# The first two fifths of W_qkv split inside the last tile of the cross stage, in a shared buffer; W_o loads moved to later steps

## The chip, the cores and the metric

The kernel runs on one core of a Trainium2 chip. A time is the device time of one execution in microseconds; several executions are compared by their median. The engines are TensorE (PE), VectorE (DVE), ScalarE (ACT), GpSimd (POOL) and SyncE (SP, which here only issues DMAs and waits). The 16 DMA engines are shared by the queues that SP, ACT and POOL issue on.

## The reference

A decoder block on x (16 x 64 tokens, width 512), in float32: cross attention to a context, causal self attention, and a mixture of experts, each behind a layernorm and with a residual. Cut to the parts that matter here:

```python
def xattn(hq, kv_c):                      # 16 heads, context 1024 x 128
    q_r = einsum(einsum((hq @ Wq.T), w_kc_q), W_qr)
    kv_rope = kv_c * cos + rotate_half(kv_c) * sin
    attn = softmax(q_r @ (kv_rope @ W_kr).T)
    return ((attn @ kv_rope) @ w_kc_kv) @ Wo.T
def attn(h):                              # 32 query heads, 4 key/value heads of 64
    q, k, v = split(h @ w_qkv.T)          # w_qkv: (32 + 2 * 4) * 64 rows x 512
    q, k = rope(q), rope(k)
    return softmax(causal(q @ k.T * 64 ** -0.5)) @ v @ w_o.T
x = x + xattn(layernorm(x), ctx)
x = x + attn(layernorm(x))
x = x + moe(layernorm(x))                 # 16 experts, top 4 in 2 of 4 groups, and a shared one
```

## The kernel before, in words

The 1024 tokens are 8 tiles of 128 (two batches each). Four stages follow each other, each in a block of its own: every engine has a program of its own there, and all engines meet at the end of a block. `build_queries` folds the weights of the cross attention, `build_cross` does the cross attention and the layernorm behind it, `build_self` the self attention, `build_moe` the output projection and the experts. Products are made in three matmuls (`mm3`) of an upper and a lower float32r part. A `Pair` is such a split: ACT casts the raw data to the upper part, DVE or POOL subtracts it from the raw data for the lower one.

**The cross stage.** A tile is worked in four quarters c = 0 to 3 (two batches, two halves of the heads). In a quarter TensorE goes through k = 0 to 7: it turns the probabilities of key tile k into the PSUM banks psTr, two in turn; ACT casts them to the upper part (L653), DVE makes the lower part and so frees the bank (L700); two steps later TensorE multiplies them with the values (psV). Between these stand scores of the next quarter, where there is one, and heads of the output projection (psX). In the last quarter of the last tile there are no more scores, and behind its steps come heads 4 to 15, the residual, the layernorm of the last tile, its turn (L818), the cast and the store of h2 (L631). ACT issues the stores of x1 and h2. SP loads contexts and queries and fills the scatter area `xs` with zeros, 18 fills of 8 blocks. The last four fills are issued after the last tile's x load, and behind them, on the same queue, the loads of chunks 0 and 1 of W_qkv into the buffer `early`. At the end of its program ACT waits until all stores of x1 and h2 have landed.

**The self stage.** W_qkv has five chunks of 512 columns: chunk 0 for keys and values, 1 to 4 for the queries of four groups of heads. `high(c)` on ACT and `low(c)` on DVE split them. Chunk c + 1 is wanted by the c-th of the first steps. A step works one group of heads of one tile: products for three steps ahead, rope (three terms on DVE, a sum on POOL), the turn of the queries, scores, exponentials, the turn of the probabilities and the values. 32 steps are worked, the first 8 and the last 8 written out. SP loads h2 transposed (HT), the tables, chunks 2 to 4, and then chunks of W_o into the same raw buffers `ahead`, each behind the splitting of the chunk that lies there.

Of the kernel before, what the change touches and what calls it, by code (L numbers as in the profile page):

```python
# [29 lines left out]
P = 128  # L30
# [23 lines left out]


# [13 lines left out]
class Pair:  # L69
# [48 lines left out]
def build_queries(nc, ctx, sem, t, keep):  # L118
# [9 lines left out]
    WB = [Pair(ctx, nc, f"wb{j}", [P, W_B]) for j in range(2)]  # L128
    TW = sb("tw", [P, 2, R])
    C = Pair(ctx, nc, "cfold", [P, KC, P])  # L130
    Q = Pair(ctx, nc, "qr", [P, T])
# [73 lines left out]
    def _(pool):  # L205
# [25 lines left out]
    def _(act):  # L231
        def split_high(j, n):
            act.wait_ge(w_in[j], 16 * n)
            act.copy(WB[j].hi[:], raw[j][:, W_A:]).then_inc(wB_hi, 1)

# [183 lines left out]
TURN_H2_AT = (3, 2)  # L419

# [28 lines left out]
def build_cross(nc, ctx, sem, t, keep):  # L449
# [8 lines left out]
    KV = [Pair(ctx, nc, f"kv{j}", [P, LT, DC]) for j in range(2)]  # L458
    KT = [Pair(ctx, nc, f"kT{j}", [P, L]) for j in range(2)]
    QE = [ctx.enter_context(nc.sbuf_tensor(f"qe{j}", [P, 2, H * S], F32R)) for j in range(2)]  # L460
    PR = [sb(f"probs{j}", [P, RT, L]) for j in range(2)]
    PT = [Pair(ctx, nc, f"probsT{j}", [P, BANK]) for j in range(PTN)]
    CT = Pair(ctx, nc, "ctxT", [P, H, P])
# [25 lines left out]
    x1_out, h2_out = sem("x1_out"), sem("h2_out")  # L489
# [18 lines left out]

    block = ctx.enter_context(nc.Block())

    @block.sync
    def _(sp):
# [7 lines left out]
        def load_qe(b, j):  # L520
            sp.dma_start(QE[j][:].bitcast(F32), qe_d[b]).then_inc(qe_in[j], 16)
# [77 lines left out]
    def _(act):  # L599
# [4 lines left out]
        def kv_high(b, j):  # L604
            act.wait_ge(rope_done, b + 2)
            act.copy(KV[j].hi[:].rearrange("p l d -> p (l d)"), kr[j]).then_inc(kv_hi, 1)
# [76 lines left out]
        act.wait_ge(x1_out, 16 * NT + 16)  # L683
        act.wait_ge(h2_out, 16 * NT + 16)

    @block.vector
    def _(dve):
# [42 lines left out]

        def lo_k(j, q, count, slot):
# [146 lines left out]
WCH = 5  # L878
GI = 2 * HKV


def build_self(nc, ctx, sem, t, keep):
# [5 lines left out]
    W = Pair(ctx, nc, "wqkv", [P, WCH, KC, BANK])  # L888
    raw = keep["early"] + keep["ahead"][:WCH - 2]
    tab = sb("rope_s_tab", [P, 2, 3, DH // 2])  # L890
    mask_f, mask = sb("mask_f", [P, BANK]), sb("mask_r", [P, BANK], F32R)
    ident_r = sb("ident_r", [P, P], F32R)
    HT = [sb(f"h2T{j}", [P, 2, KC, P], F32R) for j in range(2)]
# [8 lines left out]
    VB = [Pair(ctx, nc, f"v_pairs{j}", [P, 2, HKV, 2, DH]) for j in range(2)]  # L902
    PR = [sb(f"sprobs{j}", [P, REP, S]) for j in range(2)]
    PT = [Pair(ctx, nc, f"sprobsT{j}", [P, REP // 2, P]) for j in range(2)]
# [14 lines left out]
    ht_in = [sem(f"ht_in{j}") for j in range(2)]  # L919
    w_hi, w_ready = sem("wqkv_hi"), sem("wqkv_ready")  # L920
# [39 lines left out]
    def _(sp):  # L960
        sp.dma_start(HT[0][:].bitcast(F32).rearrange("p a k x -> p a (k x)"), t["h2T"][0]).then_inc(ht_in[0], 16)
        sp.dma_start(tab[:], t["rope_s"]).then_inc(tab_in, 16)
        sp.dma_start(mask_f[:], t["mask"]).then_inc(tab_in, 16)
        for c in range(2, WCH):
            sp.dma_start(raw[c], t["w_qkv"][c]).then_inc(w_in[c], 16)
        sp.dma_start(HT[1][:].bitcast(F32).rearrange("p a k x -> p a (k x)"), t["h2T"][1]).then_inc(ht_in[1], 16)
        for c in range(W_AHEAD):
            if c < WCH - 2:
                sp.wait_ge(w_ready, c + 3)
            sp.dma_start(keep["ahead"][c], t["w_o"][:, c * KC:(c + 1) * KC, :]).then_inc(wo_in[c], 16)  # L970

# [66 lines left out]
    def _(act):  # L1038
        def high(c):
            act.wait_ge(w_in[c], 16)  # L1040
            act.copy(W.hi[:, c], raw[c]).then_inc(w_hi, 1)
# [38 lines left out]
        high(3)  # L1080
# [5 lines left out]
        def step(i, v, last):  # L1086
# [19 lines left out]
    def _(dve):  # L1106
# [21 lines left out]
        def low(c):  # L1128
            dve.wait_ge(w_hi, c + 1)
            dve.tensor_tensor(W.lo[:, c], raw[c], f32(W.hi[:, c]), ALU.subtract).then_inc(w_ready, 1)  # L1130
# [18 lines left out]
        low(0)  # L1149
        low(1)  # L1150
# [1029 lines left out]
```

## Time and profile before

| | us |
|---|---|
| median of 3 runs | 1498.34 (1495.42 to 1498.8) |
| the profiled execution | 1496.33 |
| its span | 1494.4 |
| PE busy | 1355.5 (91%) |
| DVE busy | 800.7 (54%) |
| ACT busy | 737.9 (49%) |
| POOL busy | 573.0 (38%) |

The span is from the first to the last instruction of the profiled execution, so it is a little under its time. The cross stage ends and the self stage begins at about 785 us of the span. Times in the rows are us from the span's start.

### The profile page before, as it was taken

To read this page: it belongs to the slowest core of one execution; us is meant where nothing else is said; L and a number is where in the kernel's file an instruction comes from. 1 tells how busy PE (TensorE), PEld (TensorE's weight loads), DVE (VectorE), ACT (ScalarE), POOL (GpSimd) and SP (SyncE) were. 2 spreads that over 40 slices of the span, in tenths; PEclk is the share of its full clock that TensorE was granted. 3 is DMA by queue.
4 is the path that set the end of the run, shared out by engine and by line. 5 is a ranking of instruction groups with operands and counts; after the bars stand their busy time and mean duration, and the time that the engine had idled before them with its cause. 6 is when DMAs were issued, how large, how long until landed. Compare 5 with 4: busy or idle time off the path is not lost. (4 is left out here: it accounts for less than half of the span.)

```text
span 1494.4 us, 22780 instructions
## 1 busy us (share of the span) xinstructions
PE 1355.5 (91%) x7136; PEld 1109.7 (74%) x7136; DVE 800.7 (54%) x1371; ACT 737.9 (49%) x1741; POOL 573.0 (38%) x346
## 2 busy tenths in 40 slices
PE   5998699999999999999975999998689989999992
PEld 4776577878787878787854888887578768787772
DVE  4444366666666666666634445444479853432226
ACT  2444465565656565656524677777432214333331
POOL 2430133233332323232003333333346486427975
PEclk9999799999999999999997999999699999999997
DMA  5785414141414141413094111112643256536667
GB/s 195 262 269 178 172 50 149 54 173 50 175 49 175 48 177 43 182 42 113 1 330 178 64 64 50 50 50 99 225 146 132 78 184 225 174 121 224 233 201 232
DMA packets 78984, 209.79 MB, mean 140 GB/s; under 512 B 5888, under 2 KB 39168, under 8 KB 72960
## 3 DMA queue, kind: packets, MB, share of 16 engines
q1 hardware_dynamic: 69472, 163.78, 31.7%
q0 software_dynamic: 7136, 38.80, 7.6%
q10 hardware_dynamic: 2304, 6.29, 1.1%
q8 instruction: 40, 0.66, 0.2%
q14 instruction: 32, 0.26, 0.1%
HBM read 154.59 MB, written 92.01 MB: 165 GB/s over the span
## 5 line engine op out<-in xcount | busy, mean ns | idle before, releaser
L700 DVE TENSOR_TENSOR probsT_lo<-psTr,probsT_hi 128x512 fp32r<-128x512 f32 x256 | 176.7, 690 | 168.0 <-ACT probsT_hi L653 167.7
L653 ACT CAST probsT_hi<-psTr 128x512 fp32r<-128x512 f32 x256 | 150.1, 587 | 199.0 <-PE psTr L784 195.3
L784 PE MATMUL psTr<-ident,probs 128*128 128x128 f32 x1024 | 153.6, 274 | 11.3 <-DVE probsT_lo L700 5.2
L784 PEld LDWEIGHTS psTr<-ident,probs 128*128 128x128 f32 x1024 | 124.3, 141 | 50.4 <-DVE probsT_lo L700 13.5
L695 DVE TENSOR_REDUCE nmax<-psS 128x1 f32<-128x1024 f32 x128 | 155.5, 1215 | 9.5 <-PE psS L66 8.4
L610 ACT ACTIVATE probs<-psS,nmax 128x1024 f32<-128x1024 f32 x128 | 143.8, 1123 | 12.2 <-DVE nmax L695 12.2
L566 POOL TENSOR_TENSOR ctxT_lo<-ctx_f,ctxT_hi 128x512 fp32r<-128x512 f32 x32 | 41.4, 1295 | 278.0 <-ACT ctxT_hi L617 278.0
L64 PE MATMUL bank<-w_slots,ao_first_hi 128*128 (+1 forms) x252 | 108.5, 430 | 16.2 <-DVE w_slots L1807 9.6
L64 PE MATMUL psS<-kT_hi,qe 128*128 128x512 f32 x256 | 113.0, 441 | 3.7 <-DMA qe<-qe 2.8
L64 PE MATMUL psV<-probsT_hi,kv_hi 128*128 128x512 f32 x256 | 114.7, 448 | 0.6
L1513 POOL TENSOR_TENSOR w_slots<-w_ahead,w_slots 128x3072 fp32r<-128x3072 f32 x15 | 102.1, 6809 | 1.2
L66 PE MATMUL psS<-kT_hi,qe 128*128 128x512 f32 x256 | 102.1, 399 | 0.0
L65 PE MATMUL psS<-kT_lo,qe 128*128 128x512 f32 x256 | 101.5, 397 | 0.0
L66 PE MATMUL psV<-probsT_hi,kv_lo 128*128 128x512 f32 x256 | 101.1, 395 | 0.0
L66 PE MATMUL bank<-w_slots,ao_first_lo 128*128 (+1 forms) x252 | 100.4, 398 | 0.0
L65 PE MATMUL bank<-w_slots,ao_first_hi 128*128 (+1 forms) x252 | 100.4, 398 | 0.0
L65 PE MATMUL psV<-probsT_lo,kv_hi 128*128 128x512 f32 x256 | 100.2, 392 | 0.0
L64 PE MATMUL bank<-w_slots 128*128 128x512 f32 (+1 forms) x206 | 84.5, 410 | 7.1 <-DVE w_slots L1863 4.2
L1863 DVE TENSOR_TENSOR w_slots<-bank,w_slots 128x256 fp32r<-128x256 f32 x47 | 20.0, 425 | 122.6 <-ACT w_slots L1641 118.6
L1219 PEld LDWEIGHTS psSs<-kTs,qT 128*128 128x128 f32 x512 | 75.9, 191 | 9.6
L65 PE MATMUL bank<-w_slots 128*128 128x512 f32 (+1 forms) x206 | 81.6, 396 | 0.0
L66 PE MATMUL bank<-w_slots 128*128 128x512 f32 (+1 forms) x206 | 81.6, 396 | 0.0
(273 smaller groups left out, 3323.8 us busy)
## 6 DMA issues: line engine op xcount, KB each, us to landing
w_ahead<-w_exp POOLq DMA_DIRECT2D x14, 1536.0 KB, 7.4
qe<-stage SPq DMA_DIRECT2D x16, 1024.0 KB, 6.8
qe<-qe SPq DMA_DIRECT2D x16, 1024.0 KB, 5.0
wraw<-w_pairs SPq DMA_DIRECT2D x8, 1792.0 KB, 11.5
early<-xs SPq DMA_DIRECT2D x47, 256.0 KB, 2.7
xs<-h_rows SPq DMA_DIRECT2D x47, 256.0 KB
early<-ctx SPq DMA_DIRECT2D x16, 512.0 KB, 11.6
ao<-attn_out SPq DMA_DIRECT2D x32, 256.0 KB, 2.4
```

The source lines that it names most:

```text
L64: pe.matmul(out, lhs[0], rhs[0], start=start, stop=False, skip_group_check=True)
L65: pe.matmul(out, lhs[0], rhs[1], start=False, stop=False, skip_group_check=True)
L66: return pe.matmul(out, lhs[1], rhs[0], start=False, stop=stop, skip_group_check=True)
L566: pool.tensor_tensor(CT.lo[:, cols[0], cols[1]], CX[:].rearrange("p (h s) -> p h s", s=S), f32(CT.hi[:, cols[0], cols[1]]), ALU.subtract). ...
L610: act.activation(PR[np_][:, rt, :], psS[rt % 2][:], ACT.Exp, bias=nmax[np_][:, rt:rt + 1], accum_out=rsum[np_][:, rt:rt + 1]).then_inc(exp ...
L653: act.copy(PT[k % PTN].hi[:], psT[slot][:]).then_inc(turned_hi, 1)
L695: dve.tensor_reduce(nmax[np_][:, rt:rt + 1], psS[rt % 2][:], AX.X, ALU.max, negate=True).then_inc(max_made, 1)
L700: dve.tensor_tensor(out, psT[slot][:], f32(hi), ALU.subtract).then_inc(turned_free, 1)
L784: last = pe.transpose(psT[slot][:, q * P:(q + 1) * P], src(q), ident[:])
L1219: last = pe.matmul(psS[j][:, h, :], QB[j][:, h].rearrange("p b s -> p (b s)"), KB[kt][:, g, :], start=False, stop=h == REP - 1, skip_group ...
L1513: pool.tensor_tensor(slot(e)[1], raw[(e + 1) % 2], f32(slot(e)[0]), ALU.subtract).then_inc(w_ready, 1)
L1863: dve.tensor_tensor(HT[i % 2][1], psHT[i % 2][:, 0:I].rearrange("p (k x) -> p k x", k=NIT), f32(HT[i % 2][0]), ALU.subtract).then_inc(ht_l ...
```

## The change

One buffer, `w_slots`, is now allocated for the whole kernel, and the float32r data of the first three stages (F, h1T, queries, keys, KV, the context; then W_qkv's parts, HT, the V and probability parts, the mask) are given places in it. When the last scores are done the queries' and keys' places are dead, and chunks 0 and 1 of W_qkv are split into them: ACT casts them in the last quarter of the last tile behind its casts for k = 3 and k = 5, DVE subtracts behind its lower parts for k = 4 and k = 6. Then SP loads chunks 2 and 3 into `early`, and before them the first two tiles of HT. ACT doesn't wait any more for the stores of x1 and h2 at the end of the stage; the waits stand later, ahead of the first maximum on DVE, in the second step on SP and ACT, and in `build_moe`. In the self stage ACT and DVE begin with chunk 2, and one split fewer stands among the first products. The W_o chunks are loaded at steps 2, 4 and 6.

The core of the diff:

```diff
@@ build_cross
+W_STEPS = (3, 5)
+    W = [Shared(ws, c * WSZ, (KC, BANK)) for c in range(2)]
+    HT = [ws[:, AT_KV + j * HTZ:AT_KV + (j + 1) * HTZ] for j in range(2)]
+    w_in, w_hi, w_ready = keep["wqkv_in"], keep["wqkv_hi"], keep["wqkv_ready"]
@@ SP, end of its program
         sp.dma_start(keep["early"][1], t["w_qkv"][1]).then_inc(keep["wqkv_in"][1], 16)
+        sp.wait_ge(pv_done, LT * (HB * NT - 1))
+        sp.wait_ge(h2_out, 16 * 3)
+        for j in range(2):
+            sp.dma_start(f32(HT[j]), h2_d[j].rearrange("p a x -> p (a x)")).then_inc(keep["ht_in"][j], 16)
+        for j in range(2):
+            sp.wait_ge(w_ready, j + 1)
+            sp.dma_start(keep["early"][j], t["w_qkv"][2 + j]).then_inc(w_in[2 + j], 16)
@@ ACT
+        def wqkv_high(c):
+            act.wait_ge(s_mm, RT * HB * NT)
+            act.wait_ge(w_in[c], 16)
+            act.copy(W[c].hi, keep["early"][c]).then_inc(w_hi, 1)
@@
                     if k % 2 == 1 and more:
                         exps(n + 1, (c + 1) % 2, k // 2)
+                    if not more and k in W_STEPS:
+                        wqkv_high(W_STEPS.index(k))
                     if not first:
                         if (c, k) == (2, 7):
                             store_x1(i - 1)
@@
         store_h2(NT - 1)
-        act.wait_ge(x1_out, 16 * NT + 16)
-        act.wait_ge(h2_out, 16 * NT + 16)
@@ DVE
+        def wqkv_low(c):
+            dve.wait_ge(w_hi, c + 1)
+            dve.tensor_tensor(W[c].lo, keep["early"][c], f32(W[c].hi), ALU.subtract).then_inc(w_ready, 1)
@@
                         maxes(n + 1, (c + 1) % 2, k // 2)
+                    if not more and k - 1 in W_STEPS:
+                        wqkv_low(W_STEPS.index(k - 1))
@@ build_self
-    raw = keep["early"] + keep["ahead"][:WCH - 2]
+    raw = keep["early"] + keep["early"] + keep["ahead"][:1]
@@ SP
-        sp.dma_start(HT[0][:].bitcast(F32).rearrange("p a k x -> p a (k x)"), t["h2T"][0]).then_inc(ht_in[0], 16)
         sp.dma_start(tab[:], t["rope_s"]).then_inc(tab_in, 16)
         sp.dma_start(mask_f[:], t["mask"]).then_inc(tab_in, 16)
-        for c in range(2, WCH):
-            sp.dma_start(raw[c], t["w_qkv"][c]).then_inc(w_in[c], 16)
-        sp.dma_start(HT[1][:].bitcast(F32).rearrange("p a k x -> p a (k x)"), t["h2T"][1]).then_inc(ht_in[1], 16)
-        for c in range(W_AHEAD):
-            if c < WCH - 2:
-                sp.wait_ge(w_ready, c + 3)
-            sp.dma_start(keep["ahead"][c], t["w_o"][:, c * KC:(c + 1) * KC, :]).then_inc(wo_in[c], 16)
+        sp.dma_start(raw[4], t["w_qkv"][4]).then_inc(w_in[4], 16)
         def step(i, v, last):
             u, tt, g, ahead = plan(i, v, last)
+            if isinstance(u, int) and u in WO_STEPS:
+                c = WO_STEPS.index(u)
+                if c == 0:
+                    sp.wait_ge(w_ready, WCH)
+                sp.dma_start(keep["ahead"][c], t["w_o"][:, c * KC:(c + 1) * KC, :]).then_inc(wo_in[c], 16)
@@ ACT
-        high(0)
-        high(1)
+        high(2)
         act.wait_ge(tab_in, 32)
-        act.copy(mask[:], mask_f[:]).then_inc(consts, 1)
-        act.copy(ident_r[:], ident[:]).then_inc(consts, 1)
-        high(2)
+        act.copy(mask, mask_f[:]).then_inc(consts, 1)
+        act.copy(ident_r, ident[:]).then_inc(consts, 1)
+        high(3)
         act.wait_ge(zeroed, 6)
         turned(order_k(0), KB[0], HKV)
         turned(order_q(0, 0), QB[0], REP)
-        high(3)
         exps(0, 0)
@@ DVE
-        low(0)
-        low(1)
+        low(2)
         dve.wait_ge(tab_in, 32)
         terms_k(0)
         terms_q(0)
-        low(2)
+        low(3)
         terms_q(1)
-        low(3)
+        dve.wait_ge(keep["x1_out"], 16 * NT + 16)
         maxes(0, 0)
```

## Rows read from the trace of the kernel before

**Rows 1.** The page, TensorE: busy us (share of the span), instructions.
```profile
PE 1355.5 (91%) x7136; PEld 1109.7 (74%) x7136; DVE 800.7 (54%) x1371; ACT 737.9 (49%) x1741; POOL 573.0 (38%) x346
```

**Rows 2.** Windows at the seam: busy us (instructions) by engine, clock, DMA share, GB/s.
```profile
760.00:765.00 5.00, 5.00 (x28) 4.11 (x27) 2.08 (x3) 1.59 (x3) 0.00 (x0) 1.00 1.23 429
...
770.00:775.00 5.00, 5.00 (x23) 4.12 (x23) 0.00 (x0) 0.00 (x0) 0.00 (x0) 1.00 0.83 257
775.00:780.00 5.00, 1.61 (x7) 0.79 (x5) 2.27 (x5) 0.05 (x1) 0.55 (x1) 0.84 0.99 416
780.00:785.00 5.00, 0.00 (x0) 0.00 (x0) 0.69 (x1) 0.54 (x1) 0.00 (x0) 0.50 0.51 208
...
790.00:795.00 5.00, 5.00 (x13) 3.91 (x12) 1.54 (x2) 2.59 (x3) 0.48 (x1) 0.50 0.99 415
```

**Rows 3.** Timeline, TensorE, 759 to 810: start, us, what [idle before].
```profile
759.19 0.60 PE L784 MATMUL psTr<-ident,probs 128*128 128x128 f32 x4
...
775.11 0.39 PE L66 MATMUL psX<-F_hi,ctxT_lo 128*128 128x512 f32 x1
...
789.36 0.80 PE L64 MATMUL psK<-wqkv_hi,h2T 128*128 128x512 f32 x1 [9.49 <-DVE wqkv_lo L1130]
...
795.07 0.58 PE L65 MATMUL psQs<-wqkv_lo,h2T 128*128 128x512 f32 x1
...
797.79 0.38 PE L1203 MATMUL psTk<-ident,k_rope 128*128 128x128 f32 x2
802.71 1.12 PE L1203 MATMUL psTq<-ident,q_rope 128*128 128x128 f32 x4 [4.54 <-POOL q_rope L1021]
...
805.33 0.57 PE L65 MATMUL psQs<-wqkv_lo,h2T 128*128 128x512 f32 x1
...
807.60 1.89 PE L1219 MATMUL psSs<-kTs,qT 128*128 128x64 f32 x16
```

**Rows 4.** Timeline, ScalarE and its queue, 757 to 789.
```profile
757.54 0.59 ACT L653 CAST probsT_hi<-psTr 128x512 fp32r<-128x512 f32 x1 [0.48 <-PE psTr L784]
...
759.83 0.35 ACTq L631 DMA_DIRECT2D h2T<-h2T_tile  x1
...
781.30 0.34 ACTq L631 DMA_DIRECT2D h2T<-h2T_tile  x1
785.08 3.70 ACT L1041 CAST wqkv_hi<-early 128x2048 fp32r<-128x2048 f32 x2 [4.54 <-PEq L2080]
```

**Rows 5.** DMA issues by line, two windows: KB each, us to landing.
```profile
early<-w_qkv SPq DMA_DIRECT2D x1, 1024.0 KB, 30.8
xs<-zeros SPq DMA_DIRECT2D x1, 27.8
...
h2T<-h2T_tile ACTq DMA_DIRECT2D x1, 512.0 KB, 3.3
```

**Rows 6.** Timeline, SP's queue, at the last fills.
```profile
747.04 2.43 SPq L524 DMA_DIRECT2D xs<-zeros  x4
749.51 0.58 SPq L549 DMA_DIRECT2D early<-w_qkv  x1
```

**Rows 7.** DMA queues, 750 to 780, ACT's queue: packets, MB, share of 16 engines.
```profile
q10 hardware_dynamic: 301, 0.81, 7.1%
```

**Rows 8.** Timeline, VectorE, 758 to 811.
```profile
758.16 0.69 DVE L700 TENSOR_TENSOR probsT_lo<-psTr,probsT_hi 128x512 fp32r<-128x512 f32 x1 [0.27 <-ACT probsT_hi L653]
...
808.84 2.28 DVE L1130 TENSOR_TENSOR wqkv_lo<-w_ahead,wqkv_hi 128x2048 fp32r<-128x2048 f32 x1
```

**Rows 9.** Timeline, GpSimd, 789 to 803.
```profile
789.53 0.95 POOL L1002 MEMSET v_pairs_lo<- 128x1024 f32 x1
795.86 0.74 POOL L1007 TENSOR_TENSOR k_rope<-k_terms 128x256 f32<-128x256 f32 x1 [5.38 <-DVE k_terms L1116]
799.42 3.24 POOL L1021 TENSOR_TENSOR q_rope<-q_terms 128x512 f32<-128x512 f32 x1 [2.82 <-DVE q_terms L1116]
```

**Rows 10.** Window in the self stage, columns as in rows 2.
```profile
840.00:860.00 20.00, 19.78 (x132) 17.38 (x132) 10.09 (x22) 15.67 (x71) 6.89 (x7) 1.00 0.11 41
```

More of the change, by code:

```diff
@@ L53 @@
 W_AHEAD = HQ * DH // P // KC - 1
+AT_QE, AT_KEYS = 0, 4 * H * S
+AT_F = AT_KEYS + 4 * L
+AT_KV = AT_F + 2 * H * D
+AT_CT = AT_KV + 4 * LT * DC
+WS_ALL = AT_CT + 2 * H * P
+WCH = 5
+WSZ = 2 * KC * BANK
+HTZ, VBZ = 2 * KC * P, 8 * HKV * DH
+AT_CONST = WCH * WSZ
+AT_VB = AT_KV + 2 * HTZ
+AT_PT = AT_VB + 2 * VBZ
+assert AT_CONST + BANK + P <= AT_KV and AT_PT + 2 * REP * P <= WS_ALL
+assert 4 * W_B + 2 * T <= WS_ALL - AT_KV
 NE, TOPK, NG, TOPG, I = 16, 4, 4, 2, 256
@@ L77, in at, with __init__, shaped @@
         return self.hi[idx], self.lo[idx]
+class Shared(Pair):
+    def __init__(self, ws, at, dims):
+        n = int(np.prod(dims))
+        self.hi, self.lo = (shaped(ws[:, at + j * n:at + (j + 1) * n], dims) for j in range(2))
+def shaped(ap, dims):
+    names = "abcd"[:len(dims)]
+    return ap.rearrange(f"p ({' '.join(names)}) -> p {' '.join(names)}", **dict(zip(names, dims)))
 def f32(ap):
@@ L127, in build_queries @@
     raw = [sb(f"wraw{j}", [P, W_A + W_B]) for j in range(2)]
-    WB = [Pair(ctx, nc, f"wb{j}", [P, W_B]) for j in range(2)]
+    WB = [Shared(keep["ws"], AT_KV + 2 * j * W_B, (W_B,)) for j in range(2)]
     TW = sb("tw", [P, 2, R])
     C = Pair(ctx, nc, "cfold", [P, KC, P])
-    Q = Pair(ctx, nc, "qr", [P, T])
+    Q = Shared(keep["ws"], AT_KV + 4 * W_B, (T,))
     stage = sb("stage", [P, 2, T * 2])
@@ L233, in split_high @@
             act.wait_ge(w_in[j], 16 * n)
-            act.copy(WB[j].hi[:], raw[j][:, W_A:]).then_inc(wB_hi, 1)
+            act.copy(WB[j].hi, raw[j][:, W_A:]).then_inc(wB_hi, 1)
         def fold_t(q):
@@ L457, in build_cross @@
     kv, kr = keep["kv_raw"], keep["kv_rope"]
-    KV = [Pair(ctx, nc, f"kv{j}", [P, LT, DC]) for j in range(2)]
-    KT = [Pair(ctx, nc, f"kT{j}", [P, L]) for j in range(2)]
-    QE = [ctx.enter_context(nc.sbuf_tensor(f"qe{j}", [P, 2, H * S], F32R)) for j in range(2)]
+    ws = keep["ws"]
+    KV = [Shared(ws, AT_KV + 2 * j * LT * DC, (LT, DC)) for j in range(2)]
+    KT = [Shared(ws, AT_KEYS + 2 * j * L, (L,)) for j in range(2)]
+    QE = [shaped(ws[:, AT_QE + 2 * j * H * S:AT_QE + 2 * (j + 1) * H * S], (2, H * S)) for j in range(2)]
     PR = [sb(f"probs{j}", [P, RT, L]) for j in range(2)]
     PT = [Pair(ctx, nc, f"probsT{j}", [P, BANK]) for j in range(PTN)]
-    CT = Pair(ctx, nc, "ctxT", [P, H, P])
+    CT = Shared(ws, AT_CT, (H, P))
     CX = sb("ctx_f32", [P, BANK])
@@ L605, in kv_high @@
             act.wait_ge(rope_done, b + 2)
-            act.copy(KV[j].hi[:].rearrange("p l d -> p (l d)"), kr[j]).then_inc(kv_hi, 1)
+            act.copy(KV[j].hi.rearrange("p l d -> p (l d)"), kr[j]).then_inc(kv_hi, 1)
         def exps(n, np_, rt):
@@ L877 @@
 NGRP = NT * HKV
-WCH = 5
 GI = 2 * HKV
+WO_STEPS = (2, 4, 6)
 def build_self(nc, ctx, sem, t, keep):
@@ L886, in sb @@
         return ctx.enter_context(nc.sbuf_tensor(name, shape, dt))
-    W = Pair(ctx, nc, "wqkv", [P, WCH, KC, BANK])
-    raw = keep["early"] + keep["ahead"][:WCH - 2]
+    ws = keep["ws"]
+    W = [Shared(ws, c * WSZ, (KC, BANK)) for c in range(WCH)]
+    raw = keep["early"] + keep["early"] + keep["ahead"][:1]
     tab = sb("rope_s_tab", [P, 2, 3, DH // 2])
-    mask_f, mask = sb("mask_f", [P, BANK]), sb("mask_r", [P, BANK], F32R)
-    ident_r = sb("ident_r", [P, P], F32R)
-    HT = [sb(f"h2T{j}", [P, 2, KC, P], F32R) for j in range(2)]
+    mask_f, mask = sb("mask_f", [P, BANK]), ws[:, AT_CONST:AT_CONST + BANK]
+    ident_r = ws[:, AT_CONST + BANK:AT_CONST + BANK + P]
+    HT = [shaped(ws[:, AT_KV + j * HTZ:AT_KV + (j + 1) * HTZ], (2, KC, P)) for j in range(2)]
     QR = sb("q_terms", [P, 2, BANK])
@@ L900, in build_self @@
     KB = [sb(f"kTs{j}", [P, HKV, S]) for j in range(2)]
-    VB = [Pair(ctx, nc, f"v_pairs{j}", [P, 2, HKV, 2, DH]) for j in range(2)]
+    VB = [Shared(ws, AT_VB + j * VBZ, (2, HKV, 2, DH)) for j in range(2)]
     PR = [sb(f"sprobs{j}", [P, REP, S]) for j in range(2)]
-    PT = [Pair(ctx, nc, f"sprobsT{j}", [P, REP // 2, P]) for j in range(2)]
+    PT = [Shared(ws, AT_PT + j * REP * P, (REP // 2, P)) for j in range(2)]
     AO = [sb(f"attn_out{j}", [P, BANK]) for j in range(2)]
@@ L918, in build_self @@
     tab_in = sem("tabs_in")
-    ht_in = [sem(f"ht_in{j}") for j in range(2)]
-    w_hi, w_ready = sem("wqkv_hi"), sem("wqkv_ready")
+    ht_in, w_hi, w_ready = keep["ht_in"], keep["wqkv_hi"], keep["wqkv_ready"]
     zeroed, consts = sem("zeroed"), sem("consts")
@@ L1040, in high @@
             act.wait_ge(w_in[c], 16)
-            act.copy(W.hi[:, c], raw[c]).then_inc(w_hi, 1)
+            act.copy(W[c].hi, raw[c]).then_inc(w_hi, 1)
         def turned(order, dst, n):
@@ L1098, in step @@
                 exps(u + 1, (v + 1) % 2)
+            if isinstance(u, int) and u == 1:
+                act.wait_ge(keep["h2_out"], 16 * NT + 16)
             if not (isinstance(u, int) and u == 0):
@@ L1129, in low @@
             dve.wait_ge(w_hi, c + 1)
-            dve.tensor_tensor(W.lo[:, c], raw[c], f32(W.hi[:, c]), ALU.subtract).then_inc(w_ready, 1)
+            dve.tensor_tensor(W[c].lo, raw[c], f32(W[c].hi), ALU.subtract).then_inc(w_ready, 1)
         def maxes(u, j):
@@ L1185, in product @@
             for k in range(KC):
-                last = mm3(pe, out, (HT[j][:, 0, k, :], HT[j][:, 1, k, :]), W.at(ALL, c, k, ALL),
+                last = mm3(pe, out, (HT[j][:, 0, k, :], HT[j][:, 1, k, :]), W[c].at(ALL, k, ALL),
                            k == 0, k == KC - 1)
@@ L1214, in scores_mask @@
             wait(pe, exp_done, REP * (u - 1))
-            pe.matmul(psS[j][:], ident_r[:], mask[:], start=True, stop=False, skip_group_check=True)
+            pe.matmul(psS[j][:], ident_r, mask, start=True, stop=False, skip_group_check=True)
         def scores(g, j, kt, heads):
@@ L1382, in build_moe @@
     psD, psG, psXT, psHT = pb[2:4], pb[6:8], pb[4:6], pb[0:2]
-    WO = [WS[:, j * nh * D:(j + 1) * nh * D].rearrange("p (h x) -> p h x", x=D) for j in range(2)]
+    WO = [Shared(WS, c * WSZ, (KC, D)) for c in range(nh // KC)]
     a1 = 2 * nh * D
@@ L1585, in wo_high @@
             act.wait_ge(wo_in[c], 16)
-            act.copy(WO[0][:, c * KC:(c + 1) * KC, :], wo_raw[c]).then_inc(wo_hi, 1)
+            act.copy(WO[c].hi, wo_raw[c]).then_inc(wo_hi, 1)
         def h3_high(tt):
```

33 lines of the change are left out of this document (18 added, 15 removed).

## The prediction

> **What bounds the kernel now.** I read the page's busy shares first, then the windows around the seam between the cross stage and the self stage, then the timelines of the five engines there, and last the landing times of the DMAs. TensorE is busy for 91% of the span [rows 1]; so outside the seam a microsecond counts if TensorE loses it. In the seam the windows show it: 5.00 of 5 us before 775, 1.61 to 780, nothing to 785, and a clock of 0.50 behind that [rows 2]. The timelines say what it waits for. The last projection starts at 775.11 and ends at 775.5; then come the residual, the layernorm, the turn and the store of the last h2 tile, issued at 781.30 [rows 4]. It lands 3.3 us later [rows 5], at 784.6, the scalar engine waits for that, and its first cast of the self stage starts at 785.08. Two casts (3.70 us) and behind the first a subtraction stand ahead of the first product at 789.36 [rows 3, 4].
>
> One more thing is to be read before the change is costed: when the raw W_qkv chunks are there. SP issues chunk 0 at 749.51 and it lands 30.8 us later, at 780.3; chunk 1, of the same 1.05 MB, is queued right behind it [rows 5, 6]. Ahead of both in the same queue stand the last four zero fills of xs, issued from 747.04 on [rows 6], 2.10 MB each (8 x 128 x 512 x 4 bytes), 8.39 MB in all; the last landed 27.8 us after its issue near 748.9, at 776.7 [rows 5]. In the kernel before nobody sees this, because the chunks are wanted only at 785.
>
> **The change part by part.** *The early split.* In the last quarter of the last tile ScalarE casts chunk 0 right behind its cast for k=3 and chunk 1 behind that for k=5. The cast for k=4 was at 757.54 [rows 4]. Right ahead of it ScalarE now has an instruction that waits for chunk 0. It isn't there for another 22 us. SP's program up to this load is the same, so I see nothing that brings it sooner, but for one thing: the ACT queue's traffic (x1 and h2 stores). The store of h2 tile 6, issued at 759.83 [rows 4], is behind the blocked cast in program order and leaves later, and so is x1 of tile 7. The ACT queue took 7.1% of the 16 engines' time from 750 to 780 for 0.81 MB [rows 7], 2.1 us; the x1 store of tile 6, 0.26 MB, stays. Two thirds of 2.1 is 1.4; I take 1.3 us off: chunk 0 lands at 779.0.
>
> Behind it on ScalarE are the cast for k=4, the reciprocal row copy, the casts for k=5, 6, 7 and both stores. DVE's lower part of k=4 waits for the cast, TensorE's turn k=5 (759.19 before) waits for DVE to free the bank, so TensorE has the matmuls up to 759.2 and then stops. New times: cast of chunk 0 at 779.1, next instruction 1.8 us on (half of 3.70 for two [rows 4]), k=4's cast at 780.9, DVE 0.62 later (758.16 against 757.54), 0.69 long [rows 8], so the turn of k=5 at 782.3 against 759.19: **+23.1**.
>
> *The second chunk* is there 3 to 4 us behind the first (1.05 MB at near 290 GB/s, the rate of this queue) and ScalarE comes to it at 783.8, so its wait costs nothing. Its 1.9 us lie beside the values of k=3, head 0 and the turn of k=6 on TensorE, 3 us at the low clock. DVE's subtractions (2.28 each [rows 8]) begin at 782.1 and 787.8; the lower part of k=5 slips to 784.4 and is wanted by the turn of k=7 near 788. Nothing for these three; with that cover gone it would be up to 1.8 us.
>
> *The clock.* After 23 us of idling TensorE starts at 0.50. In this trace a start from 0.50 stayed slow from 789.36 to about 795.3 and from 802.71 to 805.5 [rows 3]. At the low level 13 matmuls fit in 5 us against 23 at the high one [rows 2], so a slow stretch loses 0.44 to 0.46 of its length: 1.3 to 2.7, I take **+1.8**. From there 15.9 us of work follow as before (759.19 to 775.11), until 800.0.
>
> *The end of the stage.* ScalarE no longer waits for the stores to land: from the end of the store's issue (781.64) to the next stage was 3.4 us, of which 0.4 from the landing on is the barrier and stays: **-3.0**. The stage seam falls at about 807.0 instead of 785.1.
>
> *The first self loads and products.* The first product starts at the seam instead of 4.3 us behind it. The products for K and Q took 8.4 us from 789.36 to 797.79, at a clock that is low at the start again. Then DVE's three terms, POOL's sum (799.42, 3.24 us long [rows 9]) and the turn at 802.71, 17.65 us behind the seam [rows 3]. Now 0.1 + 8.4 + 1.65 + 3.24 + 0.1 = 13.5: **-4.1**. POOL's sum stays at 3.24 us, because one subtraction still runs beside it on DVE, for chunk 3 where it was chunk 2. The others are ready: chunks 2 and 3 are loaded from 784 and 790 on, into buffers whose splitting ends then; the six memsets end 5.4 us behind the seam and POOL's sum for K, 6.5 us behind the first product's start, comes 6.6 behind it [rows 9].
>
> *One subtraction less before the first maximum.* Scores end at 809.49 [rows 3]; DVE is done with its terms at 808.8, then subtracts for 2.28 us and takes the maximum only near 811.1 [rows 8]. Now it can at 809.5: **-1.5**. The exponentials, the values' split, the last subtraction and the first step follow each other from there, so it stays.
>
> *The W_o loads* leave at the third, fifth and seventh step of the self stage, where the 16 DMA engines are 11% busy in a window of 20 us [rows 10], and are wanted only after the self stage: nothing. The new waits for x1 and h2 stores stand before the first maximum and at the second step; the last h2 store landed in 3.3 us [rows 5] and these places are more than 20 us behind the seam: nothing. The shared buffer moves addresses, not work.
>
> Sum: 23.1 + 1.8 - 3.0 - 4.1 - 1.5 = **+16.3**. The profiled execution took 1496.33 us around a span of 1494.4; it gives 1512.6. The median of the runs is 2.0 higher, which gives 1514.6; I say 1514.
>
> Here a rule of the Trainium skill can be set beside the rows. The rows show chunk 0 landing 3.6 us behind the last fill, and 8.39 + 1.05 MB and an x tile passing in 33 us, near 290 GB/s. "DMA: Bandwidth & Descriptors", Queues, rings and completion order, says that each engine consumes a queue's descriptors in ring order; this trace agrees. The same page's Specifications give 435 GB/s as the ceiling of the fabric; by an estimate from it chunk 0 would land 22.3 us after 747.0, and the sum would be +6.6. The trace is slower than that, and the trace decides.
>
> **The rivals.** *The queue drains faster* (7 in 100). The best 5 us window moved 429 GB/s [rows 2]. If everything from 747.0 to chunk 0 ran like this (8.39 + 1.05 MB, 0.26 of the x tile, 0.26 of an x1 store, 9.96 in all), chunk 0 would be there at 770.2: 8.8 us less, +7.5, 1505. For it: the engines' own reads and writes stop while they wait. Against it: a window of 257 GB/s among the same traffic [rows 2], with DVE and ScalarE doing nothing at all in it.
>
> *The wait is met, and it is faster* (5 in 100). If chunk 0 had landed by 757, only ScalarE's 1.8 us would sit between k=3 and k=4 and push k=4 by 1.3, and k=6 by 0.5; the gains stay: 1.8 - 3.0 - 4.1 - 1.5 = -6.8, 1491. It decides from the landing: the case breaks even where chunk 0 lands some 7 us after 757, near 764. The trace has 780.3 and the SP program is unchanged, so it needs fills that vanish from the queue. Near 764 it comes out as no change (2 in 100 more).
>
> *The gains at the seam are eaten* (10 in 100). The self stage's start is a chain through five engines; if the terms, POOL's sum or a table make it as long as before, -4.1 and -1.5 drop out, and with the slow stretch at 5.9 us the sum is 23.1 + 2.7 - 3.0 = +23, 1521.
>
> *The forecast* (76 in 100), with its own range 1510 to 1518: chunk 0 at 777.5 to 780.3 gives -1.5 to +1.3, the clock -0.5 to +0.9, the seam -1 to +1, and the runs before spread over 3.4 us (1495.42 to 1498.8).
>
> The range of 8 in 10 takes in the forecast with what lies between it and the first rival, and a little of the slow side: 1506 to 1519. A difference of 0.2% (3 us) is about what a measurement of this kernel can tell from none. Faster 0.05, same 0.02, slower 0.93.
>
> **What the profile after would show.** ScalarE waits some 22 us for DMA at the cast of chunk 0, in the last quarter of tile 7. TensorE has an idle stretch of about 23 us from 759 on, with a clock of 0.50 behind it. Chunk 0's landing is 28 to 31 us. The store of h2 tile 6 is issued near 786. The last projection ends near 800, the next stage starts within 0.5 us of the last store's issue, and the first turn of Q stands 13.5 us behind the seam. From the first steps of the self stage to the end everything is shifted by 16 us and otherwise equal. The forecast is wrong if that DMA wait is under 15 us, if the turn of k=5 doesn't hang on the cast of k=4, or if a stage far from the seam changes its length.

## The result and the profile after

| | median, us | runs |
|---|---|---|
| before | 1497.57 | 4 (1495.42 to 1498.8) |
| after | 1516.74 | 4 (1514.55 to 1520.56) |

The ratio is 1.0126, with a 95% interval of 1.0107 to 1.0145: the change makes the kernel slower by 1.3%, 19.2 us between the medians, where 16.3 were worked out and 1514 forecast. The profiled execution after took 1520.56 us, the slowest of the four, so times far from the seam are not compared between the two profiles; 1.8 us of the difference of their spans lie ahead of the last tile of the cross stage already.

The windows over the last tile and the seam, after (columns as in [rows 2]; these stand 1.8 us later on the clock of their span):

```profile
760.00:765.00 5.00, 1.20 (x7) 0.72 (x6) 0.00 (x0) 0.00 (x0) 0.00 (x0) 0.90 0.76 266
765.00:770.00 5.00, 0.00 (x0) 0.00 (x0) 0.00 (x0) 0.00 (x0) 0.00 (x0) 0.50 1.26 439
...
775.00:780.00 5.00, 0.00 (x0) 0.00 (x0) 0.00 (x0) 0.00 (x0) 0.00 (x0) 0.50 0.90 288
780.00:785.00 5.00, 0.00 (x0) 0.00 (x0) 0.25 (x1) 2.67 (x3) 0.00 (x0) 0.50 0.79 329
785.00:790.00 5.00, 4.50 (x15) 3.83 (x16) 3.24 (x3) 2.59 (x3) 0.00 (x0) 0.50 0.52 160
```

In [rows 2] TensorE is full from 760 to 765 and from 770 to 775; here it does nothing from 765 to 785, and 4.50 us of matmuls follow at a clock of 0.50. VectorE, ScalarE and GpSimd are empty as well up to 780, while the DMA engines are at 0.90 in the window from 775. That is what a wait for a transfer looks like when every engine hangs on it. ScalarE's timeline, as [rows 4], names it:

```profile
758.31 0.59 ACT L699 CAST probsT_hi<-psTr 128x512 fp32r<-128x512 f32 x1
782.33 1.90 ACT L677 CAST w_slots<-early 128x2048 fp32r<-128x2048 f32 x1 [23.43 <-DMA early<-w_qkv]
784.14 0.58 ACT L699 CAST probsT_hi<-psTr 128x512 fp32r<-128x512 f32 x1
...
786.65 0.59 ACT L699 CAST probsT_hi<-psTr 128x512 fp32r<-128x512 f32 x1 [1.45 <-PE psTr L836]
786.74 0.35 ACTq L672 DMA_DIRECT2D h2T<-h2T_tile  x1
787.13 1.90 ACT L677 CAST w_slots<-early 128x2048 fp32r<-128x2048 f32 x1
...
809.79 0.34 ACTq L672 DMA_DIRECT2D h2T<-h2T_tile  x1
810.58 1.90 ACT L1092 CAST w_slots<-early 128x2048 fp32r<-128x2048 f32 x1 [1.54 <-PEq L2131]
```

The cast of chunk 0 (L677) has been waiting for the DMA for 23.43 us, and only behind it come the cast for k=4 (784.14) and, at 786.74, the store of h2 tile 6, which was issued at 759.83 in [rows 4]. The second cast of a chunk, at 787.13, waited for nothing. The lower part of k=4 on VectorE and the turn of k=5 on TensorE follow the cast:

```profile
784.75 0.69 DVE L746 TENSOR_TENSOR probsT_lo<-psTr,probsT_hi 128x512 fp32r<-128x512 f32 x1 [25.02 <-ACT probsT_hi L699]
785.36 2.28 DVE L779 TENSOR_TENSOR w_slots<-early,w_slots 128x2048 fp32r<-128x2048 f32 x1
```

```profile
785.50 1.12 PE L836 MATMUL psTr<-ident,probs 128*128 128x128 f32 x4 [24.30 <-DVE probsT_lo L746]
...
804.12 0.39 PE L80 MATMUL psX<-w_slots 128*128 128x512 f32 x1
...
810.75 0.77 PE L78 MATMUL psK<-w_slots 128*128 128x512 f32 x1 [2.34 <-PEq L2131]
...
823.29 1.12 PE L1253 MATMUL psTq<-ident,q_rope 128*128 128x128 f32 x4 [4.55 <-POOL q_rope L1072]
...
832.05 0.66 PE L1253 MATMUL psTq<-ident,q_rope 128*128 128x128 f32 x4 [0.82 <-POOL q_rope L1063]
```

Against [rows 3], the turn of k=5 has 24.30 us of idling in front, the last projection begins at 804.12, and the first product at 810.75 is 0.17 us behind ScalarE's first cast of the new stage (810.58). In the kernel before it was 4.3 us. SP's queue and the landing of chunk 0, as [rows 5, 6]:

```profile
748.87 2.43 SPq L558 DMA_DIRECT2D xs<-zeros  x4
751.34 0.58 SPq L583 DMA_DIRECT2D early<-w_qkv  x1
...
754.19 0.80 SPq L590 DMA_DIRECT2D w_slots<-h2T  x2
```

```profile
DMA to landing us min/median/max: 30.9/30.9/30.9
```

And the ACT queue over the same 30 us as in [rows 7]:

```profile
q10 hardware_dynamic: 144, 0.26, 2.6%
```

Its share fell from 7.1% to 2.6%, as the forecast said it would. The landing did not move: 30.9 us against 30.8.

To compare kernels whose spans begin a little differently, I count from SP's last x tile load of the cross stage (746.64 before, 748.48 after). The columns are starts of instructions, but the second is the end of the last projection; the last is SP's load of HT in the second step of the self stage, behind which all kernels run alike.

| us from the x tile load | turn of k=5 | projections end | first product | first turn of Q | load in step 2 |
|---|---|---|---|---|---|
| before | 12.55 | 28.86 | 42.72 | 56.07 | 82.30 |
| after | 37.02 | 56.03 | 62.27 | 74.81 | 102.06 |

The last column differs by 19.8, and the medians by 19.2, so the difference of the medians arises here. The spans of the two profiles differ by 24.3: 1.8 ahead of the x tile load, 19.8 here, and 2.7 behind. The rest of the self stage, up to the load of W_o that begins the next stage, takes 229.4 to 230.3 us in the profiles of all kernels here, so neither the later W_o loads nor the shared buffer cost anything there. What follows takes 435.2 us in the profile before and 438.4 after, but 439.0 in e6 below, whose code in that stage is that of the kernel before: single executions differ by that much.

### The profile page after: what moved, and what is told of

Its sections match the earlier page's. It is cut to its first block and busy times, and to the rows that moved or that the text cites. A ratio compares the mean times of both kernels' runs of the same rounds, so it can differ in the third digit from the quotient of the medians.

```text
span 1518.7 us, 22796 instructions
## 1 busy us (share of the span) xinstructions
PE 1359.1 (89%) x7136; PEld 1112.5 (73%) x7136; DVE 802.1 (53%) x1371; ACT 737.0 (49%) x1741; POOL 572.2 (38%) x346
## 5 line engine op out<-in xcount | busy, mean ns | idle before, releaser
L607 POOL TENSOR_TENSOR w_slots<-ctx_f,w_slots 128x512 fp32r<-128x512 f32 x32 | 41.3, 1291 | 305.2 <-ACT w_slots L658 305.2
L78 PE MATMUL psV<-probsT_hi,w_slots 128*128 128x512 f32 x256 | 115.4, 451 | 0.6
L78 PE MATMUL psS<-w_slots 128*128 128x512 f32 x256 | 112.2, 438 | 3.8 <-DMA w_slots<-qe 2.9
L80 PE MATMUL psV<-probsT_hi,w_slots 128*128 128x512 f32 x256 | 101.5, 397 | 0.0
L80 PE MATMUL psS<-w_slots 128*128 128x512 f32 x256 | 101.5, 397 | 0.0
L79 PE MATMUL psV<-probsT_lo,w_slots 128*128 128x512 f32 x256 | 100.7, 393 | 0.0
L79 PE MATMUL psS<-w_slots 128*128 128x512 f32 x256 | 100.7, 393 | 0.0
## 6 DMA issues: line engine op xcount, KB each, us to landing
early<-ctx SPq DMA_DIRECT2D x16, 512.0 KB, 11.3
```

The lines of the kernel that those rows point to most:

```text
L78: pe.matmul(out, lhs[0], rhs[0], start=start, stop=False, skip_group_check=True)
L79: pe.matmul(out, lhs[0], rhs[1], start=False, stop=False, skip_group_check=True)
L80: return pe.matmul(out, lhs[1], rhs[0], start=False, stop=stop, skip_group_check=True)
L607: pool.tensor_tensor(CT.lo[:, cols[0], cols[1]], CX[:].rearrange("p (h s) -> p h s", s=S), f32(CT.hi[:, cols[0], cols[1]]), ALU.subtract). ...
```

## The experiments

The theory: the loss is the cast of chunk 0, which stands in ScalarE's program ahead of the cast for k=4 and waits for a load that stands in SP's queue behind four zero fills. Rival 1: the inserted casts, subtractions and waits cost the time themselves. Rival 2: the shared buffer does. Each kernel was timed against the kernel before on the same chip (median of before there 1498.4 to 1498.6). The microseconds against before are the ratio's. The executions of one kernel spread over 4 to 10 us, and the difference of the medians can be another by up to 2 us (7.5 instead of 7.9 for e1, 4.1 instead of 6.3 for e2). So two kernels that differ by 1 or 2 us can't be put in order.

**e1: the chunks ahead of the fills.** Only the order in SP's program is changed:

```diff
         tiles(sp, iteration)
-        for r in range(2 * NT - 2, NBLK // NT):
-            fill(r)
         sp.wait_ge(rope_done, B + 1)
         sp.dma_start(keep["early"][0], t["w_qkv"][0]).then_inc(keep["wqkv_in"][0], 16)
         sp.wait_ge(turned, place(NT - 2, 2, "K", 1, True)[0])
         sp.wait_ge(kv_lo, B - 1)
         sp.dma_start(keep["early"][1], t["w_qkv"][1]).then_inc(keep["wqkv_in"][1], 16)
+        for r in range(2 * NT - 2, NBLK // NT):
+            fill(r)
```

> The changed kernel with the loads of chunks 0 and 1 issued ahead of the last four zero fills; nothing else. Theory (the cast of chunk 0 waits for a load that stands behind 8.4 MB of fills in the same queue): chunk 0 lands 5 to 6 us after its issue, near 753, before the cast is reached; the 24 us stall of TensorE is gone. HT, chunks 2 and 3 and the tables now stand behind the fills, so some of the gain at the seam may be lost: 2 us faster than before (5 faster to 2 slower). Rival 1 (the inserted casts and subtractions and the new waits cost the time, not the queue): still 15 to 19 us slower than before. Rival 2 (the shared buffer slows the engines' accesses): still slower as well, spread over the stages.

Measured: 1491.05 us, ratio 0.9947 (0.9929 to 0.9965), 7.9 us faster than before and some 27 faster than the change as made. That is better than the range that was expected (5 faster to 2 slower). Rivals 1 and 2 fall: everything that they blame is still in this kernel. Chunk 0's landing, and its cast on ScalarE's timeline, with no wait in front:

```profile
DMA to landing us min/median/max: 5.1/5.1/5.1
```

```profile
761.31 1.91 ACT L677 CAST w_slots<-early 128x2048 fp32r<-128x2048 f32 x1
...
787.02 0.58 ACT L668 CAST h2T_tile<-psX 128x512 fp32r<-128x512 f32 x1 [12.98 <-DMA h2T<-h2T_tile]
...
791.95 1.90 ACT L1092 CAST w_slots<-early 128x2048 fp32r<-128x2048 f32 x1 [4.34 <-DMA early<-w_qkv]
796.56 0.62 ACT L1124 CAST w_slots<-mask_f 128x512 fp32r<-128x512 f32 x1 [2.71 <-DMA mask_f<-mask]
```

The price that the expectation put on the fills now standing ahead of the other loads is there too (waits of 12.98 for the store of h2 tile 6, 4.34 for chunk 2, 2.71 for the mask), but it cost less than I had thought. In the table below the first product stands 1.8 us later than in e2, and the first turn of Q 0.6 sooner; e7 shows why.

**e2: the fills in the self stage.** The same loop of fills stands behind the load of chunk 4 in `build_self`.

> The changed kernel with the last four fills issued in the self stage, behind the load of chunk 4, so that nothing stands behind them that is wanted soon. Theory: no stall at the cast of chunk 0, only its 1.8 us push the cast for k=4 by about 1.3 us; the last store's landing (-3.5) and the shorter way to the first turn of Q (-4.9) remain: 7 us faster than before (5 to 9). Rival 1: 15 to 19 us slower. Rival 2: slower by the stages' share. A second rival to the theory's size (the gains measured at the seam exist only because the stall gave the loads time): between 3 slower and 3 faster.

Measured: 1494.43 us, ratio 0.9958 (0.9941 to 0.9975), 6.3 us faster, as expected. The gains at the seam exist without the stall. Chunk 0 lands after 5.0 us, and in front of the turn of k=5 there are 0.76 us of idling:

```profile
DMA to landing us min/median/max: 5.0/5.0/5.0
```

```profile
757.82 0.66 PE L834 MATMUL psTr<-ident,probs 128*128 128x128 f32 x4 [0.76 <-DVE probsT_lo L744]
...
777.82 0.66 PE L868 MATMUL psX<-ident,h_tile 128*128 128x128 f32 x4 [3.25 <-DVE h_tile L767]
780.82 0.77 PE L78 MATMUL psK<-w_slots 128*128 128x512 f32 x1 [2.34 <-PEq L2131]
...
793.97 1.11 PE L1253 MATMUL psTq<-ident,q_rope 128*128 128x128 f32 x4 [4.54 <-POOL q_rope L1072]
```

**e3: half the dose.** Two fills ahead of the chunks, two in the self stage.

> The changed kernel with two of the four fills ahead of the chunks and two in the self stage: half the dose. Theory: 4.2 MB less at near 290 GB/s brings the landing 14.5 us sooner and the issue 1.2 us; the stall shrinks from 24.5 to about 9 us and the whole comes to 3 us slower than before (1 faster to 6 slower), between the other two. Rival 1: no different from the changed kernel, 15 to 19 slower. A threshold (the queue only stalls above some load) would give either of the ends.

Measured: 1503.53 us, ratio 1.0031 (1.0018 to 1.0045), 4.6 us slower, between the ends.

```profile
DMA to landing us min/median/max: 18.4/18.4/18.4
```

```profile
764.88 1.90 ACT L677 CAST w_slots<-early 128x2048 fp32r<-128x2048 f32 x1 [9.64 <-DMA early<-w_qkv]
```

```profile
768.04 1.11 PE L836 MATMUL psTr<-ident,probs 128*128 128x128 f32 x4 [10.51 <-DVE probsT_lo L746]
```

With 0, 2 and 4 fills ahead, chunk 0 lands 5.0, 18.4 and 30.9 us behind its own issue, and the idle time in front of the turn of k=5 is 0.76, 10.51 and 24.30. The dose shows no threshold. For what a fill costs, the issue of the chunk is the wrong start: it slips with the fills ahead, and they drain from their own issue on. Counted from the x tile load the landings are at 5.4, 20.0 and 33.8 us: 7.1 us for a fill of 2.10 MB, near 296 GB/s, and near the 290 of the prediction. That is also why I had 9 us for the middle one. I took 14.5 us off for two fills and 1.2 more for their issue, which is no time of its own; the stall shrank by 13.8.

**e4: the shared buffer alone.** All splits, loads and waits are put back where the kernel before has them; the data stay at their new places.

> Only the shared buffer of the change: all splits, loads and waits where the kernel before has them. Theory: no difference from before (within 1.5 us), stage by stage. Rival 2 (the places of the data cost time): slower by several us, visible as longer matmuls, casts or subtractions in the cross stage.

Measured: 1498.95 us, ratio 1.0004 (0.9991 to 1.0017): no difference. The split of the probabilities, 256 times in the cross stage, is as long as in the kernel before (690 and 587 ns on its page):

```profile
L739 DVE TENSOR_TENSOR probsT_lo<-psTr,probsT_hi 128x512 fp32r<-128x512 f32 x256 | 176.7, 690 | 168.1 <-ACT probsT_hi L692 167.8
...
L692 ACT CAST probsT_hi<-psTr 128x512 fp32r<-128x512 f32 x256 | 150.1, 587 | 198.9 <-PE psTr L827 195.2
```

**e5: no wait at the stage's end.** e4 without ScalarE's last two waits:

```diff
         store_h2(NT - 1)
-        act.wait_ge(x1_out, 16 * NT + 16)
-        act.wait_ge(h2_out, 16 * NT + 16)
```

> The kernel with the shared buffer alone (e4), and besides it only this of the change: ScalarE doesn't wait at the end of the cross stage for the stores of x1 and h2. Theory: the seam moves 3.3 to 3.5 us ahead, as after the change (6.46 us from the last projection to the self stage's first cast against 9.97), and nothing takes it back: 3 us faster than before (1 to 4). Rival (the seam's gain is lost, since the first self loads wait for HT, which is loaded only there): within 1 us of before.

Measured: 1498.03 us, ratio 0.9993 (0.9981 to 1.0004). A miss: 3 us were expected, and the interval takes in 0 (2.8 faster to 0.6 slower). The stage does end 3 us sooner, but the first product then waits for HT, as the rival had it:

```profile
777.20 1.12 PE L859 MATMUL psX<-ident,h_tile 128*128 128x128 f32 x4 [3.25 <-DVE h_tile L760]
786.26 0.77 PE L78 MATMUL psK<-w_slots 128*128 128x512 f32 x1 [7.95 <-DMA w_slots<-h2T]
```

HT is loaded from the seam on, and the product starts 5.8 us behind the issue. Against the kernel before, the first product gained 1.6 us (41.15 in the table below against 42.72), and 0.8 are left at step 2. e4, the kernel that differs in the two waits alone, gives a wider distance (43.60 and 84.81), but its profiled execution took 1501.46 us, 2.5 over its median, with longer stretches at the low clock. So dropping the end wait paid in full only together with loads that stand ahead of the seam, which the change has.

**e6: the kernel before with late fills.** A control for e2.

> The kernel before with its last four zero fills issued in the self stage, behind the loads of HT and of chunks 2 to 4; nothing else. A control: if the fills by themselves cost or give time, what e2 gained isn't the change's. Theory: the chunks aren't wanted before the seam here, so 0 (1.5 faster to 1 slower; the stores of x1 and h2 land sooner without the fills, which may give some tenths). Rival (the fills slow the last tile of the cross stage by their traffic, whatever the split does): 4 to 7 us faster.

Measured: 1498.36 us, ratio 0.9989 (0.9975 to 1.0003); the way up to step 2 is as long as before (82.36 against 82.30), though the seam stood 1.1 us sooner (37.28 against 38.42). The 4 to 7 us of the rival lie outside the interval (3.7 faster to 0.4 slower), so what e2 gained is not the fills' place by itself; a part of it can be.

**e7: chunk 3 sooner.** On e2, `high(3)` directly behind `high(2)` and `low(3)` directly behind `low(2)`.

> The kernel with the fills in the self stage (e2), and chunk 3's cast and subtraction directly behind chunk 2's, so that no subtraction of DVE runs beside GpSimd's sum for the first queries. In e1, where chunk 3 came late, that sum took 1.26 us; in e2, with the subtraction beside it, 3.24. Theory (the two disturb each other): the sum takes 1.3 us here, the first turn of Q stands 10.8 us behind the seam instead of 13.3, and the kernel is 1.9 us faster than e2: 8 us faster than before (6.5 to 10). Rival (the first sum is slow for another reason, a first use): the sum stays at 3.2 us and the kernel within 1 us of e2.

Measured: 1491.55 us, ratio 0.9954 (0.9939 to 0.9969), against e2's 0.9958. The subtraction on VectorE and GpSimd's sum for the first queries, in e2:

```profile
790.52 2.28 DVE L1181 TENSOR_TENSOR w_slots<-early,w_slots 128x2048 fp32r<-128x2048 f32 x1
```

```profile
790.68 3.24 POOL L1072 TENSOR_TENSOR q_rope<-q_terms 128x512 f32<-128x512 f32 x1 [2.66 <-DVE q_terms L1167]
```

The sum in e7, with no subtraction near it:

```profile
797.11 1.26 POOL L1072 TENSOR_TENSOR q_rope<-q_terms 128x512 f32<-128x512 f32 x1 [1.97 <-DVE q_terms L1167]
```

The disturbance is shown: 3.24 us for the sum behind a subtraction that began 0.16 us sooner, 1.26 without, with the same data. The expectation had e1's case wrong in one thing. There the subtraction did run beside the sum, but began 0.50 us behind it, and then the sum took 1.26 and the subtraction 2.92 instead of 2.28:

```profile
798.72 1.26 POOL L1072 TENSOR_TENSOR q_rope<-q_terms 128x512 f32<-128x512 f32 x1 [0.53 <-DVE q_terms L1167]
```

```profile
799.22 2.92 DVE L1181 TENSOR_TENSOR w_slots<-early,w_slots 128x2048 fp32r<-128x2048 f32 x1 [0.57 <-ACT w_slots L1092]
```

So in both orders the one that began second took longer. The worth of this is not shown: the first turn of Q stands 11.3 us behind the seam instead of 13.4, but at step 2 only 1.1 of the 2.1 us are left, and the two kernels' times can't be told apart. The other 1.0 went to the clock: 0.3 up to the product behind the idle stretch (18.74 us from the turn against 18.47), and 0.7 behind it, where the low stretch is longer (817.16 to about 823.5, against 812.44 to about 817.3 in e2). e7's timeline around the turn:

```profile
798.42 0.66 PE L1253 MATMUL psTq<-ident,q_rope 128*128 128x128 f32 x4 [2.56 <-POOL q_rope L1072]
...
799.39 0.41 PE L80 MATMUL psQs<-w_slots 128*128 128x512 f32 x1
...
800.02 0.63 PE L79 MATMUL psQs<-w_slots 128*128 128x512 f32 x1
...
801.73 0.63 PE L80 MATMUL psQs<-w_slots 128*128 128x512 f32 x1
...
803.26 0.39 PE L1265 MATMUL psSs<-w_slots 128*128 128x512 f32 x1
```

TensorE comes to the turn with the high clock, after 2.56 us of idling, and is at the low one from 799.6 to 803.0, in the middle of its work. It's the same work in e2, where the low stretch is from 793.97 to 796.7.

**e8: the casts behind the last store.** All four fills ahead of the chunks, but the splits at the end of both programs:

```diff
-                    if not more and k in W_STEPS:
-                        wqkv_high(W_STEPS.index(k))
...
         store_h2(NT - 1)
+        for c in range(2):
+            wqkv_high(c)
```

> The changed kernel with all four fills ahead of the chunks, as it is, but the casts of chunks 0 and 1 stand at the end of ScalarE's program of the cross stage, behind the last store, and the subtractions at the end of DVE's. The landing stays late; only what stands behind the wait is another. Theory (the loss is what is queued behind the waiting cast): the chunks have landed when the casts are reached, no stall in the last tile, seam near where it was before, and the rest of the gains: 3 us faster than before (1 to 5). Rival (the late landing costs in any place): 10 us or more slower.

Measured: 1497.44 us, ratio 0.9993 (0.9978 to 1.0007). The stall is gone with the landing as late as ever (31.3 us), so the late landing costs only where its wait has something behind it; the rival's 10 us are excluded. But of the 3 us of gain 1.0 is measured, which can't be told from 0:

```profile
779.04 0.58 ACT L668 CAST h2T_tile<-psX 128x512 fp32r<-128x512 f32 x1 [12.11 <-DMA h2T<-h2T_tile]
...
780.82 3.70 ACT L677 CAST w_slots<-early 128x2048 fp32r<-128x2048 f32 x2 [1.19 <-DVE h2T_tile L773]
790.25 1.90 ACT L1092 CAST w_slots<-early 128x2048 fp32r<-128x2048 f32 x1 [5.73 <-DMA early<-w_qkv]
```

The splits now lengthen the stage (its end is at 42.74, where e2's is at 36.3), the h2 cast waits for the store of tile 6, which the fills slow, and chunk 2 for its load. Here the split is a gain only where it lies beside TensorE's work.

The table for all, in the order of the last column:

| us from the x tile load | turn of k=5 | projections end | first product | first turn of Q | load in step 2 | time against before, us |
|---|---|---|---|---|---|---|
| after | 37.02 | 56.03 | 62.27 | 74.81 | 102.06 | +19.2 |
| e3, two fills | 23.23 | 42.08 | 48.49 | 60.87 | 87.93 | +4.6 |
| e4, buffer alone | 12.57 | 28.87 | 43.60 | 56.52 | 84.81 | +0.6 |
| e6, before, late fills | 12.54 | 28.85 | 41.57 | 54.25 | 82.36 | -1.6 |
| before | 12.55 | 28.86 | 42.72 | 56.07 | 82.30 | 0 |
| e8, casts last | 12.54 | 28.82 | 42.94 | 54.92 | 81.66 | -1.0 |
| e5, no end wait | 12.54 | 28.83 | 41.15 | 53.58 | 81.47 | -1.0 |
| e2, no fills | 13.49 | 30.24 | 36.49 | 49.64 | 74.98 | -6.3 |
| e1, chunks first | 13.49 | 30.24 | 38.33 | 49.04 | 74.74 | -7.9 |
| e7, chunk 3 sooner | 13.48 | 30.23 | 36.48 | 47.55 | 73.86 | -6.9 |

The last column is the ratio less one, times 1498.4 (for after the difference of the medians). It follows the one before it within 2 us: what these kernels differ in is decided in this stretch. Each row is one execution, and some of them lie well over their kernel's median (e1's took 1498.4 us, with its x tile load 4.4 us later than before's), so 1 or 2 us in a column aren't a difference between kernels.

## Why the prediction came out as it did

The mechanism was right, and each step can be laid beside the profile after. The sum came out 3 us short of the medians. By the profile it is 3.5 us short, 1.4 of them in the landing and most of the rest in the clock.

*The landing and the stall: +24.5, forecast +23.1.* Shown by e1, e2, e3 and e8 from both sides: take the fills away, or take the wait from in front of the cast for k=4, and it is gone. The 1.4 us are the term that I took off for the ACT queue's missing stores. The stores were indeed missing (2.6% instead of 7.1%), and chunk 0 landed 33.8 us behind the x tile load, against 33.7 before. So the share that a queue has of the engines' time could not simply be taken off another queue's landing. That the stores are worth nothing isn't shown either: the change also puts 1.05 MB of HT behind the chunks on SP's queue, and e8, which has these loads and the stores at their old place, lands at 34.2; e4 and e5, with the stores and without the HT loads, at 34.6 and 33.3. The Trainium skill, "DMA: Bandwidth & Descriptors", Queues, rings and completion order, says that each DMA engine consumes a queue's descriptors in ring order; the landings at 5.4, 20.0 and 33.8 us agree with it. The estimate from the ceiling of 435 GB/s that the Trainium skill gives in Specifications of the same page, +6.6, was far off. So was the rival with the queue at the 429 GB/s of its best window. A fill copies from DRAM to DRAM, and near 296 GB/s is what a row of them reached here.

*The second chunk: nothing, forecast nothing.* Its cast at 787.13 waited for nothing.

*The clock after the stall: +2.7, forecast +1.8* (19.01 us from the turn of k=5 to the last projection's end, against 16.31). The low stretch lasted from 785.50 to about 791.3, near the upper of the two bounds (2.7). In e2, without stall, the same way takes 16.75, so some 0.4 of it may be the chunks' casts and not the clock.

*The end of the stage: -3.5, forecast -3.0* (804.51 to 810.58 against 775.50 to 785.08). The 3.0 are the wait for the stores. The other 0.5 are the clock again: the turn of the last tile took 0.66 us at the high level (807.75) where it had taken 1.11 (778.75). Alone, in e5, the missing wait left 0.8 us of gain at step 2, and none that the times can tell.

*To the first turn of Q: -4.9, forecast -4.1* (823.29 - 810.58 = 12.71 against 17.63). The products took 7.6 us instead of 8.4, since the clock rose sooner (a low stretch of 4.4 us instead of 5.9).

*From there to step 2: +1.0, forecast -1.5.* This term came out with the wrong sign. The subtraction less is real: VectorE's timeline has the maximum 1.4 us behind the last terms' start, waiting for the scores alone:

```profile
829.91 0.75 DVE L1167 TENSOR_TENSOR q_terms<-psQs,rope_s_tab 128x256 f32<-128x256 f32 x2
831.33 0.69 DVE L1185 TENSOR_REDUCE snmax<-psSs 128x8 f32<-128x512 f32 x1 [0.68 <-PE psSs L1269]
```

In e2 the way from the first turn of Q to the product behind the idle stretch is 18.47 us against 19.99, the 1.5 that were forecast. After the change it is 19.70. The difference is the clock: the low stretch behind the first turn of Q lasted from 823.29 to 828.6 here, from 802.71 to 805.5 before; the one at the first step from 842.99 to 849.3 against 822.70 to about 826. That is 2.5 and 3 us more at the low level, of which 0.46 are lost: 2.5 us. The low start at 812.29 before, which has none to match it after (832.05 is at the high level), doesn't count: from the first maximum to the product behind the idle stretch it is 11.67 us before and 11.66 after. The prediction gave the clock a term for the stall and left the starts behind it (810.75, 823.29 and 842.99) as they had been.

Together 24.5 + 2.7 - 3.5 - 4.9 + 1.0 = +19.8. The misses of +1.4, +0.9, -0.5, -0.8 and +2.5 make the 3.5 us between it and 16.3; the last four, +2.1 in all, are the clock. These lengths are of one execution of each kernel, so how much of the +2.5 belongs to the change and how much to the execution isn't shown.

What stays open: why the clock's low stretches are of such different length (2.7 to 6.3 us for starts from the low level in much the same code). The runs show it and don't explain it; nothing here varied it alone. It limits what can be said of changes of 1 us in this stretch, e7's among them.

## What to carry to other kernels

Before an instruction is moved ahead, look when its data land, not when their load is issued: a load that was issued 35 us before its use and looked free stood behind 8.4 MB of zero fills in the same queue, and the wait came to light with the move. An engine that works in program order, as ScalarE did here, passes such a wait on to all that stands behind it; work that nobody wants yet should not stand in front of work that the critical engine wants in a microsecond, unless its data are surely there. The cure was the order of the issues: with the chunks ahead of the fills (e1), the same change is 7.9 us faster than before instead of 19 slower.

## What the runs showed of the hardware that I had not expected

Zero fills of 2.10 MB from DRAM to DRAM drained at 7.1 us each when queued in a row (near 296 GB/s; landings at 5.4, 20.0 and 33.8 us with 0, 2 and 4 of them ahead). With two thirds of another queue's traffic beside them gone (0.81 to 0.26 MB in 30 us), and with 1.05 MB more behind them in their own, the landing was the same within 0.1 us. GpSimd's sum of two 128 x 512 operands took 1.26 us alone and 3.24 when it began 0.16 us behind a subtraction on VectorE; in e1, where it was first by 0.50 us, the subtraction took 2.92 instead of 2.28. The Trainium skill, "SBUF — State Buffer", Terms, says that the two engines share a port pair which one instruction holds to its end while the other blocks; these two cases agree with it. TensorE's granted clock fell in the middle of a product in e7 (799.6 to 803.0), 1.2 us after it had resumed from 2.56 us of idling at the high level. So a high clock at the first matmul behind a pause didn't mean that the work behind it stayed at that clock; that the pause was the reason isn't shown.
